# A recurrent layer on one core: the vector engine's mixing-matrix product put ahead of the convolution taps in two steps of every block, and one scan moved from step 123 to step 125

## The chip, the cores and the metric

One core of a Trainium2 chip runs the whole program; the other cores are idle. The metric is the device time in microseconds. The kernel before took 1806.57 us (median of 3 runs, 1805.43 to 1807.76). A difference under 0.2%, 3.6 us, is not told from no change.

## What is computed

Two batches of 1024 tokens with 512 features are normalised, go through a state-space layer (64 heads of 64, state 128, 8 groups) and are gated by a small linear layer. Cut to what matters:

```python
xn = layernorm(x)
gate, hbc, dt = split(xn @ in_proj_w.T)
xBC = silu(conv_bias + sum(pad(hbc)[:, k:k + L] * conv_weight[:, k] for k in range(4)))
x_, B, C = split(xBC)
# step over tokens
state = state * exp(softplus(dt + dt_bias) * A)[..., None, None] + dtx[..., None] * B
y = einsum('bhpn,bhn->bhp', state, C)
# then
yn = rms_norm_per_group(y + x_ * D) * norm_weight * silu(gate)
s = yn @ out_proj_w.T
out = x + s * silu(xn @ W.T + bias + lora(xn))
```

## The kernel before

The recurrence is computed in chunks of 128 tokens: inside a chunk by a mixing matrix, between chunks through the state. A chunk of one group of 8 heads is a **step**; there are N = 128 of them (2 batches x 8 groups x 8 chunks), numbered `i`. Eight steps make one group of heads. Four steps make a **block** of 512 tokens (CPB = 4), the unit of the convolution. TAIL is 124, the first step of the last block.

Every engine's program is one written-out loop over `i`, and each engine works through its own in order, waiting on named semaphores. Nothing reorders them.

What one step holds, by engine (the lines are those of the profile):

- **TensorE (PE)**: the output projection `output` of step i-2 (12 matmuls into `ps_out`), the products L1448 and L1453 that make y of chunk i-1 from its mixing matrix M (`decay`, or `stage` for three of the last chunks) and from the state, the product of B and C into `ps_g` (L1273, L1274), 12 matmuls of a convolution tile, 12 of a gate tile, the state update `ps_s` (L1485), in most steps 12 matmuls of a second convolution tile, and four transposes (L1367).
- **VectorE (DVE)**: `scan` (L990, the running products of the decays, with a small product L997 for the last column), `dtx` and `xw` (L1030, L1038), the sums on y, state and output (L1043, L1049, L1056, L1082), `ynt_lo` (L1086), `taps` (three L875 for one convolution tile) and `mixing_matrix` (L1011: the scanned decays times `ps_g`, which gives M).
- **ScalarE (ACT)**: `conv`, the first tap of a tile and its bias (L643; in the second block of a group of heads with three single columns L642 ahead of it, in the first with a copy of three columns L627), `silu` of the finished tile (L649), the square of y (L793), `ynt_hi` (L809), the gate's silu (L707) and splits of weights. From step 120 on it makes `dtx` and `xw` as well (L770, L799).
- **GpSimd (POOL)**: the products with C (`cpre`, L1203), sums of squares, state decay (L1250), skip (L1258), rest of the weight splits.

The six convolution tiles of the next block are made in the four steps r = i % 4 of the present one. `conv_early(i)` is tile 1, 3, 5 in r = 1, 2, 3, and `conv_late(i)` is tile 0, 2, 4 in r = 0, 1, 2. For each tile PE makes 12 matmuls, ACT the first tap (semaphore `tap0`), DVE three further taps (`taps`), ACT the silu. The early tile's taps stand at the end of DVE's step i, the late tile's at the start of its step i+1. On ACT the silu of the early tile is the last thing in step i, and the first tap of the late tile is the first in step i+1.

In the four steps 0 to 3 of a group of heads the convolution tiles are those of its second block (with the edge columns L642); this text calls them an **edge block**. Steps 4 to 7 make those of the next group's first block (L627): a **plain block**.

In DVE's program M of step i came last, behind the early taps, up to step TAIL. The three last chunks 125, 126, 127 (AHEAD) have their decays in rooms of `stage`, and their scans stand in earlier steps: 127 in step 120, 125 in step 122, 126 in step 123.

Of the kernel before, what the change touches and what calls it, by code (L numbers as in the profile page):

```python
# [22 lines left out]
CPB = BLK // P  # L23
# [8 lines left out]
N = NB * CPB  # L32
# [5 lines left out]
TAIL = N - CPB  # L38
# [25 lines left out]
def inner(i):  # L64

    return (NCH - 1) * (i // NCH) + min(i % NCH, NCH - 2) + 1
# [30 lines left out]
def conv_early(i):  # L97

    nb, r = i // CPB + 1, i % CPB
    return nb * MT + 2 * r - 1 if r and nb < NB else None  # L100
# [49 lines left out]
def by_head(ap):  # L150
    return ap.rearrange("p (h c) -> p h c", h=GH)


def build(nc, hidden, w_in_t, conv_w, conv_b, dt_bias, a_log, d_skip, norm_w, w_out_t,
          lora_a, lora_b_t, w_ffn_t, ffn_bias, lora_w, out):
    ctx = ExitStack()
    with ctx:
# [137 lines left out]
        def decay_room(i):  # L295

            if i in AHEAD:
                at = AHEAD.index(i)
                return stage[1][:, GH * P:] if at == 0 else stage[0][:, (at - 1) * GH * P:at * GH * P]
            return decay[i % 3][:, :]  # L300
# [7 lines left out]
        def lasts(i):  # L308
            return (S["last_ahead"], AHEAD.index(i)) if i in AHEAD else (S["last"], inner(i))

        def scanned(i):
            return (S["scan_ahead"], AHEAD.index(i) + 1) if i in AHEAD else (S["scan"], i + 1)
# [5 lines left out]
        def last_rooms(f):  # L318

            if apart(f):  # L320
                return stage[1][:, 0:DM], stage[1][:, DM:2 * DM], S["landed_io_apart"]
            return io[:, :], x_again[:, :], S["landed_io"]
# [267 lines left out]
        def _(e):  # L590
# [160 lines left out]
            for i in range(N + DRAIN):  # L751
# [79 lines left out]
                if f is not None:  # L831
                    factor, _, landed = last_rooms(f)
                    w.wait_ge(landed, 32 * landings(f))
                    e.activation(factor, factor, ACT.Silu).then_inc(S["ffn_act"], 1)

        @block.vector
        def _(e):
# [30 lines left out]
            def taps(k):  # L868

                nb, m, blk, tile = tile_of(k)  # L870
                ps, acc = ps_conv[k % 2], xc[nb % 2][:, m, :]
                w.wait_ge(S["tap0"], k + 1)
                for d in range(1, TAPS):
                    w.wait_ge(S["taps"], taps_done(k - 1) + d - 1 if d > 1 else 0)
                    e.scalar_tensor_tensor(acc[:, d:], ps[:, 0:BLK - d], convw_sb[:, tile, TAPS - 1 - d:TAPS - d],  # L875
                                           acc[:, d:], ALU.mult, ALU.add).then_inc(S["taps"], 1)
# [76 lines left out]
            def fin(f, sums):  # L953

                acc = out_sum[:, f % NCH, :]
                factor, addend, _ = last_rooms(f)
                w.wait_ge(S["osum"], sums)
                w.wait_ge(S["ffn_act"], f + 1)
                e.tensor_tensor(acc, acc, factor, ALU.mult).then_inc(S["fin1"], 1)
                w.wait_ge(S["fin1"], f + 1)  # L960
                w.wait_ge(S["fin2"], f)
                e.tensor_tensor(acc, acc, addend, ALU.add).then_inc(S["fin2"], 1)
# [22 lines left out]
            def scan(i):  # L985

                d = decay_room(i)
                w.wait_ge(*decays_landed(i))
                w.wait_ge(S["eye"], 2)
                e.tensor_tensor_scan(d, d, eye8[:, :, :].rearrange("p h i -> p (h i)"), 0.0,  # L990
                                     ALU.mult, ALU.add).then_inc(scanned(i)[0], 1)
                if i % NCH < NCH - 1:
                    w.wait_ge(*scanned(i))
                    w.wait_ge(S["xw"], inner(i) - 1 if i <= TAIL else 0)
                    if i in AHEAD:
                        w.wait_ge(landed_prefix[i % NCH], 32)
                    e.tensor_tensor(last_room(i)[:, :, :], by_head(d)[:, :, P - 1:P], step_sizes(i).unsqueeze(2),  # L997
                                    ALU.mult).then_inc(lasts(i)[0], 1)

            def mixing_matrix(i):  # L1000
                u, d = i - DRAIN, decay_room(i)
                w.wait_ge(*scanned(i))
                w.wait_ge(S["mm_g"], i + 1)
                w.wait_ge(S["var2"], u + 1 if u >= 0 else 0)
                if i % NCH < NCH - 1:
                    w.wait_ge(S["b_tok"], inner(i))
                if i < N - 1:
                    w.wait_ge(*lasts(i))
                else:
                    w.wait_ge(S["last"], inner(TAIL))  # L1010
                e.tensor_tensor(by_head(d), by_head(d), ps_g[:, P:2 * P].unsqueeze(1).to_broadcast([P, GH, P]),  # L1011
                                ALU.mult).then_inc(S["M"], 1)

            for i in range(N + DRAIN):
# [75 lines left out]
                    fin_rest(u, f)  # L1090
                if u == N - 2:
                    fin(f, u + 1)
                if i < N and conv_early(i) is not None:
                    taps(conv_early(i))
                if i <= TAIL:
                    mixing_matrix(i)
                for k in {TAIL - 4: (N - 1,), TAIL - 2: (N - 3,), TAIL - 1: (N - 2,)}.get(i, ()):
                    scan(k)

        @block.gpsimd  # L1100
        def _(e):
# [50 lines left out]
            def fin_multiply(f):  # L1152
                b, c = f // NCH, f % NCH
                acc = out_sum[:, c, :]
                factor, _, _ = last_rooms(f)
                w.wait_ge(S["osum"], (b * GROUPS + GROUPS - 1) * NCH + c + 1)
                w.wait_ge(S["ffn_act"], f + 1)
                e.tensor_tensor(acc, acc, factor, ALU.mult).then_inc(S["fin1"], 1)
# [370 lines left out]
```

## Time and profile before

| | us |
|---|---|
| median of 3 runs | 1806.57 (1805.43 to 1807.76) |
| profiled execution, its own time | 1806.44 |
| span of its records | 1804.6 |
| PE busy | 1763.4 (98%) |
| PE weight loads busy | 1421.6 (79%) |
| DVE busy | 1522.1 (84%) |
| POOL busy | 1144.6 (63%) |
| ACT busy | 836.0 (46%) |

The profile is of one execution. Busy time is the time in which an engine has an instruction in work; ends of matmuls are modelled. "Idle before" names what an engine waited for just ahead of an instruction. The time of the profiled execution is its span and 1.8 us around it.

### The profile page before, as it was taken

To read this page: it belongs to the slowest core of one execution; us is meant where nothing else is said; L and a number is where in the kernel's file an instruction comes from. 1 tells how busy PE (TensorE), PEld (TensorE's weight loads), DVE (VectorE), ACT (ScalarE), POOL (GpSimd) and SP (SyncE) were. 2 spreads that over 40 slices of the span, in tenths; PEclk is the share of its full clock that TensorE was granted. 3 is DMA by queue.
4 is the path that set the end of the run, shared out by engine and by line. 5 is a ranking of instruction groups with operands and counts; after the bars stand their busy time and mean duration, and the time that the engine had idled before them with its cause. 6 is when DMAs were issued, how large, how long until landed. Compare 5 with 4: busy or idle time off the path is not lost.

```text
span 1804.6 us, 30682 instructions
## 1 busy us (share of the span) xinstructions
PE 1763.4 (98%) x11416; PEld 1421.6 (79%) x11416; DVE 1522.1 (84%) x1936; ACT 836.0 (46%) x1923; POOL 1144.6 (63%) x1143
## 2 busy tenths in 40 slices
PE   6999999999999999999999999999999999999997
PEld 4777888888888888888877788888888888888875
DVE  6868888888888888888888988889898888989877
ACT  4554354444435344443534444454444435444464
POOL 5428557574755757475697847648574764847466
PEclk9999999999999999999999999999999999999999
DMA  7543333233332423233564333323233332324234
GB/s 253 159 130 110 106 106 140 83 129 106 106 107 105 141 88 123 106 106 110 183 214 155 117 116 122 112 94 123 88 121 113 124 111 95 133 78 139 84 111 146
DMA packets 113508, 220.78 MB, mean 122 GB/s; under 512 B 10448, under 2 KB 46672, under 8 KB 113360
## 3 DMA queue, kind: packets, MB, share of 16 engines
q1 hardware_dynamic: 112320, 218.66, 35.7%
q8 instruction: 91, 1.49, 0.3%
q14 instruction: 57, 0.47, 0.1%
q10 hardware_dynamic: 1040, 0.16, 0.0%
HBM read 204.63 MB, written 14.16 MB: 121 GB/s over the span
## 4 chain that ended last, share of the span: by engine, by line
PE 81%; DVE 7%; ACT 4%; issue 3%; POOL 3%; DMA 1%; SPq 0%; ACTq 0%; DVEq 0%; POOLq 0%
PE ps_conv L1281 9%; PE ps_conv L1284 8%; PE ps_y L1448 6%; PE ps_conv L1287 6%; PE ps_out L1281 6%; PE ps_out L1284 6%; PE ps_gate L1281 6%; PE ps_gate L1284 6%; PE ps_y L1453 5%; PE ps_s L1485 5%; PE ps_out L1287 4%; PE ps_gate L1287 4%; PE turned_x L1367 3%; DVE xc L875 2%; PE ps_conv L1288 2%
## 5 line engine op out<-in xcount | busy, mean ns | idle before, releaser
L875 DVE SCALAR_TENSOR_TENSOR xc<-ps_conv,convw_sb,xc 128x511 f32<-128x511 f32 (+2 forms) x576 | 430.3, 747 | 154.0 <-ACT xc L643 140.5
L1214 POOL TENSOR_TENSOR rstd_col<-mean_square,half 128x1 f32<-128x1 f32 x128 | 90.1, 704 | 535.4 <-ACT mean_square L784 535.4
L990 DVE TENSOR_TENSOR_SCAN decay<-decay,eye 128x1024 f32<-128x1024 f32 x125 | 294.8, 2359 | 1.1 <-DMA decay<-decays_d 1.1
L649 ACT ACTIVATE xc<-xc 128x512 f32<-128x512 f32 x192 | 121.0, 632 | 321.9 <-DVE xc L875 320.5
L1203 POOL TENSOR_TENSOR cpre<-cpre,xc 128x1024 f32<-128x1024 f32 x112 | 268.9, 2401 | 0.0
L1281 PE MATMUL ps_conv<-xn_hi,wconv_hi 128*128 128x512 f32 x768 | 241.9, 437 | 0.0
L1284 PE MATMUL ps_conv<-xn_hi,wconv_lo 128*128 128x512 f32 x768 | 207.4, 392 | 0.0
L1448 PE MATMUL ps_y<-decay,dtx 128*64 128x128 f32 x1984 | 190.9, 279 | 3.3 <-DVE decay L1011 2.5
L1281 PEld LDWEIGHTS ps_conv<-xn_hi,wconv_hi 128*128 128x128 f32 x768 | 141.4, 194 | 49.3 <-issue 27.2
L793 ACT ACTIVATE square<-ps_y 128x512 f32<-128x512 f32 x126 | 75.6, 600 | 224.9 <-DVE ps_y L1043 224.9
L1453 PE MATMUL ps_y<-cpre,state 128*64 128x128 f32 x1760 | 171.1, 273 | 0.0
L1284 PEld LDWEIGHTS ps_conv<-xn_hi,wconv_lo 128*128 128x128 f32 x768 | 144.2, 188 | 33.0
L1287 PE MATMUL ps_conv<-xn_lo,wconv_hi 128*128 128x512 f32 x576 | 162.0, 389 | 0.0
L1448 PEld LDWEIGHTS ps_y<-decay,dtx 128*64 128x64 f32 x1984 | 117.0, 136 | 47.0 <-issue 33.4
L1281 PE MATMUL ps_out<-wout_hi,ynt_hi 128*128 128x512 f32 x512 | 150.4, 415 | 3.3 <-issue 2.1
L1011 DVE TENSOR_TENSOR decay<-decay,ps_g 128x1024 f32<-128x1024 f32 x125 | 151.3, 1210 | 0.7 <-ACT b_tok L777 0.7
L643 ACT ACTIVATE xc<-ps_conv,convb_sb,convw_sb 128x512 f32<-128x512 f32 (+1 forms) x192 | 150.8, 785 | 0.0
L1284 PE MATMUL ps_out<-wout_hi,ynt_lo 128*128 128x512 f32 x512 | 138.4, 392 | 0.0
L1281 PE MATMUL ps_gate<-xn_hi,wgate_hi 128*128 128x512 f32 x504 | 137.9, 395 | 0.0
L1258 POOL TENSOR_TENSOR skip<-xc,dskip_sb 128x512 f32<-128x512 f32 x128 | 133.3, 1042 | 5.8 <-ACT xc L649 5.8
L1284 PE MATMUL ps_gate<-xn_hi,wgate_lo 128*128 128x512 f32 x504 | 135.0, 390 | 0.0
L1086 DVE TENSOR_TENSOR ynt_lo<-ps_y,ynt_hi 128x512 fp32r<-128x512 f32 x126 | 87.1, 691 | 51.8 <-ACT ynt_hi L809 51.0
(235 smaller groups left out, 3909.0 us busy)
## 6 DMA issues: line engine op xcount, KB each, us to landing
decay<-decays_d SPq DMA_DIRECT2D x125, 512.0 KB, 5.2
cpre<-rows_d SPq DMA_DIRECT2D x112, 512.0 KB, 3.9
stage<-w_in_t SPq DMA_DIRECT2D x32, 1024.0 KB, 6.5
stage<-w_out_t SPq DMA_DIRECT2D x16, 1024.0 KB, 5.5
stage<-w_in_t SPq DMA_DIRECT2D x32, 256.0 KB, 3.2
out_sum<-hidden SPq DMA_DIRECT2D x16, 256.0 KB, 5.6
ffn_d<-sgate SPq DMA_DIRECT2D x16, 256.0 KB, 2.3
out<-out_sum SPq DMA_DIRECT2D x16, 256.0 KB, 3.1
```

The costliest lines, as they stand in the source:

```text
L643: e.activation(acc[:, first:], ps[:, first:], ACT.Identity, bias=convb_sb[:, tile, 0:1], scale=tap).then_inc(S["tap0"], 1)
L649: e.activation(xc[nb % 2][:, m, :], xc[nb % 2][:, m, :], ACT.Silu).then_inc(S["silu"], 1)
L875: e.scalar_tensor_tensor(acc[:, d:], ps[:, 0:BLK - d], convw_sb[:, tile, TAPS - 1 - d:TAPS - d], acc[:, d:], ALU.mult, ALU.add).then_inc(S ...
L990: e.tensor_tensor_scan(d, d, eye8[:, :, :].rearrange("p h i -> p (h i)"), 0.0, ALU.mult, ALU.add).then_inc(scanned(i)[0], 1)
L1011: e.tensor_tensor(by_head(d), by_head(d), ps_g[:, P:2 * P].unsqueeze(1).to_broadcast([P, GH, P]), ALU.mult).then_inc(S["M"], 1)
L1203: e.tensor_tensor(cpre[k % 2][:, :, :], cpre[k % 2][:, :, :], xc[i // CPB % 2][:, XT + 1, block_cols(i % NCH)].unsqueeze(1).to_broadcast([ ...
L1258: e.tensor_tensor(turns(skip), xc[nb % 2][:, 0:XT, block_cols(i % NCH)], dskip_sb[:, gi * XT:(gi + 1) * XT].unsqueeze(2).to_broadcast([P, ...
L1281: e.matmul(ps, a_hi(t), b_hi_(t), start=t == 0, stop=False)
L1284: e.matmul(ps, a_lo(t), b_hi_(t), start=False, stop=False)
L1287: e.matmul(ps, a_hi(t), b_lo_(t), start=False, stop=False)
L1448: mixed = e.matmul(y_h, dx[:, h * HD:(h + 1) * HD], mx[:, h * P:(h + 1) * P], start=True, stop=cm == 0, skip_group_check=True)
L1453: mixed = e.matmul(y_h, before[:, h * HD:(h + 1) * HD], c_left[:, h, :], start=False, stop=True, skip_group_check=True)
```

## The change

In steps with r = 1 and r = 2 DVE computes M before the early tile's taps, not after them. In r = 0 (no early tile) and r = 3 the order stays. And the scan of chunk 126 stands at the end of step 125 instead of step 123. No instruction is added or taken away, and the programs of the other engines are as they were.

```diff
@@ -1090,11 +1090,14 @@
                     fin_rest(u, f)
                 if u == N - 2:
                     fin(f, u + 1)
+                matrix_first = i % CPB in (1, 2)
+                if i <= TAIL and matrix_first:
+                    mixing_matrix(i)
                 if i < N and conv_early(i) is not None:
                     taps(conv_early(i))
-                if i <= TAIL:
+                if i <= TAIL and not matrix_first:
                     mixing_matrix(i)
-                for k in {TAIL - 4: (N - 1,), TAIL - 2: (N - 3,), TAIL - 1: (N - 2,)}.get(i, ()):
+                for k in {TAIL - 4: (N - 1,), TAIL - 2: (N - 3,), TAIL + 1: (N - 2,)}.get(i, ()):
                     scan(k)
```

On DVE, from the end of a step with r = 1 or 2 (`ynt_lo`) over the early taps to the late ones; before:

```order
L1086 TENSOR_TENSOR ynt_lo<-ps_y,ynt_hi 128x512
L875 SCALAR_TENSOR_TENSOR xc1<-ps_conv1,convw_sb,xc1 128x511
L875 SCALAR_TENSOR_TENSOR xc1<-ps_conv1,convw_sb,xc1 128x510
L875 SCALAR_TENSOR_TENSOR xc1<-ps_conv1,convw_sb,xc1 128x509
L1011 TENSOR_TENSOR decay1<-decay1,ps_g 128x1024
L875 SCALAR_TENSOR_TENSOR xc1<-ps_conv0,convw_sb,xc1 128x511
L875 SCALAR_TENSOR_TENSOR xc1<-ps_conv0,convw_sb,xc1 128x510
L875 SCALAR_TENSOR_TENSOR xc1<-ps_conv0,convw_sb,xc1 128x509
```

and now:

```order
L1086 TENSOR_TENSOR ynt_lo<-ps_y,ynt_hi 128x512
L1011 TENSOR_TENSOR decay1<-decay1,ps_g 128x1024
L875 SCALAR_TENSOR_TENSOR xc1<-ps_conv1,convw_sb,xc1 128x511
L875 SCALAR_TENSOR_TENSOR xc1<-ps_conv1,convw_sb,xc1 128x510
L875 SCALAR_TENSOR_TENSOR xc1<-ps_conv1,convw_sb,xc1 128x509
L875 SCALAR_TENSOR_TENSOR xc1<-ps_conv0,convw_sb,xc1 128x511
L875 SCALAR_TENSOR_TENSOR xc1<-ps_conv0,convw_sb,xc1 128x510
L875 SCALAR_TENSOR_TENSOR xc1<-ps_conv0,convw_sb,xc1 128x509
```

M (L1011) stood between the early tile's taps (`ps_conv1`) and the late tile's (`ps_conv0`); now these six stand side by side, with M ahead.

On DVE at the end of step 123 and the start of step 124; before:

```order
L1011 TENSOR_TENSOR decay0<-decay0,ps_g 128x1024
L990 SCALAR_TENSOR_TENSOR stage0<-stage0,eye8 128x1024
L997 TENSOR_TENSOR last2<-stage0,prefix_dt 128x8
L990 SCALAR_TENSOR_TENSOR decay1<-decay1,eye8 128x1024
L997 TENSOR_TENSOR last0<-decay1,prefix_dt 128x8
```

and at the end of step 125 and the start of step 126, now:

```order
L976 TENSOR_TENSOR ps_out<-ps_out,stage1 128x512
L979 TENSOR_TENSOR out_sum<-ps_out,stage1 128x512
L990 SCALAR_TENSOR_TENSOR stage0<-stage0,eye8 128x1024
L997 TENSOR_TENSOR last2<-stage0,prefix_dt 128x8
L1043 TENSOR_TENSOR ps_y<-ps_y,skip 128x512
```

L990 is the scan (the trace calls it TENSOR_TENSOR_SCAN). The scan of chunk 126 and its L997 have left the place ahead of the scan of chunk 124 (`decay1`), and stand ahead of step 126's first sum on y.

## Rows read from the trace of the kernel before

**Rows 1.** The page, part 1: busy time, share of the span, instructions

```profile
PE 1763.4 (98%) x11416; PEld 1421.6 (79%) x11416; DVE 1522.1 (84%) x1936; ACT 836.0 (46%) x1923; POOL 1144.6 (63%) x1143
```

**Rows 2.** Windows, one group: us, busy by engine, granted clock, DMA

```profile
1175.04:1280.08 105.04, 105.04 (x694) 85.09 (x693) 90.38 (x114) 47.47 (x107) 66.26 (x67) 1.00 0.33 111
```

**Rows 3.** Who waited for L1011 (M); waits of PE's weight loads: us, times, longest

```profile
  PEld ps_y L1448: 14.3, 32
...
PEld ps_y L1448 <- issue: 33.6, 94, 1.2
```

**Rows 4.** Timeline of DVE, edge block, steps 81 to 83: start, us, what

```profile
1195.14 2.31 DVE L875 SCALAR_TENSOR_TENSOR xc<-ps_conv,convw_sb,xc 128x511 f32<-128x511 f32 x3
1197.37 1.21 DVE L1011 TENSOR_TENSOR decay<-decay,ps_g 128x1024 f32<-128x1024 f32 x1
1199.55 2.32 DVE L875 SCALAR_TENSOR_TENSOR xc<-ps_conv,convw_sb,xc 128x511 f32<-128x511 f32 x3 [0.97 <-ACT xc L643]
...
1214.07 2.32 DVE L875 SCALAR_TENSOR_TENSOR xc<-ps_conv,convw_sb,xc 128x511 f32<-128x511 f32 x3 [1.29 <-ACT xc L643]
...
1226.10 1.21 DVE L1011 TENSOR_TENSOR decay<-decay,ps_g 128x1024 f32<-128x1024 f32 x1
1227.22 0.68 DVE L1030 TENSOR_TENSOR dtx<-turned_x,prefix_dt 128x512 f32<-128x512 f32 x1
```

**Rows 5.** Timeline of ACT beside it, step 81 to 82

```profile
1197.48 0.63 ACT L649 ACTIVATE xc<-xc 128x512 f32<-128x512 f32 x1 [2.49 <-DVE xc L875]
1198.02 0.82 ACT L642 ACTIVATE xc<-ps_conv,edge,convw_sb 128x1 f32<-128x1 f32 x3
1198.73 0.78 ACT L643 ACTIVATE xc<-ps_conv,convb_sb,convw_sb 128x509 f32<-128x509 f32 x1
```

**Rows 6.** Timeline of PE's weight loads: y of chunks 3, 67 and 83

```profile
170.78 0.20 PEld L1448 LDWEIGHTS ps_y<-decay,dtx 128*64 128x64 f32 x4 [0.94 <-DVE decay L1011]
...
1017.51 0.20 PEld L1448 LDWEIGHTS ps_y<-decay,dtx 128*64 128x64 f32 x4 [1.41 <-DVE decay L1011]
...
1227.59 0.20 PEld L1448 LDWEIGHTS ps_y<-decay,dtx 128*64 128x64 f32 x4 [0.35 <-DVE decay L1011]
```

**Rows 7.** Timeline of ACT, plain block: the late tiles of steps 85, 86

```profile
1251.21 0.18 ACT L627 ACTIVATE tails<-ps_conv 128x3 f32<-128x3 f32 x1 [1.17 <-PE ps_conv L1288]
...
1265.95 0.17 ACT L627 ACTIVATE tails<-ps_conv 128x3 f32<-128x3 f32 x1 [1.40 <-PE ps_conv L1288]
```

**Rows 8.** Timeline of DVE, late taps after M of steps 2, 62, 65

```profile
157.49 2.32 DVE L875 SCALAR_TENSOR_TENSOR xc<-ps_conv,convw_sb,xc 128x511 f32<-128x511 f32 x3 [0.97 <-ACT xc L643]
...
949.54 2.31 DVE L875 SCALAR_TENSOR_TENSOR xc<-ps_conv,convw_sb,xc 128x511 f32<-128x511 f32 x3 [0.83 <-ACT xc L643]
...
988.97 2.32 DVE L875 SCALAR_TENSOR_TENSOR xc<-ps_conv,convw_sb,xc 128x511 f32<-128x511 f32 x3 [1.49 <-ACT xc L643]
```

**Rows 9.** Timeline of DVE, the tail: steps 123, 124 and 126

```profile
1755.39 1.21 DVE L1011 TENSOR_TENSOR decay<-decay,ps_g 128x1024 f32<-128x1024 f32 x1
1756.52 2.28 DVE L990 TENSOR_TENSOR_SCAN stage<-stage,eye 128x1024 f32<-128x1024 f32 x1
...
1759.83 2.28 DVE L990 TENSOR_TENSOR_SCAN decay<-decay,eye 128x1024 f32<-128x1024 f32 x1
...
1785.85 0.70 DVE L976 TENSOR_TENSOR ps_out<-ps_out,io 128x512 f32<-128x512 f32 x1 [1.38 <-ACT io L834]
```

**Rows 10.** Timeline of PE, the tail: y of chunk 123, state updates 124, 125

```profile
1756.65 0.44 PE L1448 MATMUL ps_y<-decay,dtx 128*64 128x128 f32 x4 [1.00 <-DVE decay L1011]
...
1766.16 2.04 PE L1485 MATMUL ps_s<-xw,b_tok 128*128 128x512 f32 x2 [4.25 <-ACT xw L801]
...
1775.27 1.10 PE L1485 MATMUL ps_s<-xw,b_tok 128*128 128x512 f32 x2
```

**Rows 11.** Windows in the tail (columns as in rows 2)

```profile
1766.00:1768.00 2.00, 1.84 (x2) 0.73 (x3) 1.42 (x2) 1.56 (x4) 1.92 (x3) 0.50 0.00 0
```

**Rows 12.** Line L990 (the scans): shortest, median and longest, ns

```profile
L990 DVE TENSOR_TENSOR_SCAN decay<-decay,eye x125: 2277/2281/3199, 120.3 to 1759.8; 128x1024 f32<-128x1024 f32 x125
```

## The prediction

> **What bounds the kernel now.** I read the page's busy times first, then windows, then who waits for M, then the timelines of DVE, ACT and PE beside each other.
>
> PE is busy 98% of the span and DVE 84% [rows 1]. One group of heads, eight steps, takes 105.04 us, and PE is busy for all 105.04 of them [rows 2]; the group before it takes the same time. So in the middle of the program PE sets the pace.
>
> The question is how far DVE is behind it. Over the whole run PE's weight loads waited for M 14.3 us in 32 places [rows 3]. But for one, these are y of a block's fourth step (r = 3), three of which are shown [rows 6]. There PE has the least work between the step's start and its need of M, since r = 3 has no late tile. M of chunk 83 ends at 1226.10 + 1.21 = 1227.31 and the weight load for its y starts at 1227.59 [rows 4, 6]. Where PE really waits, the load starts 0.05 us after M's end: M of chunk 123 ends at 1756.60, y starts at 1756.65 [rows 9, 10]. So in an edge block DVE has 0.28 - 0.05 = 0.23 us to spare at r = 3, and no more. The reader is to see this: DVE looks idle for 16% of the time, but its chain through steps 1 to 3 of a block is as long as PE's.
>
> What does this chain consist of? In r = 1 the early taps start at 1195.14 and M at 1197.37. Then the late taps start at 1199.55, after 0.97 us of idle time that ends with ACT's first tap [rows 4]. ACT could not be sooner: the silu of the early tile starts at 1197.48, just behind the early taps, then the edge columns at 1198.02, the first tap at 1198.73, and DVE's late taps at 1199.55 [rows 5]. From the end of the early taps to the start of the late ones is 2.18 us of ACT's work, whatever DVE does meanwhile. In the kernel before, M fills 1.21 of it.
>
> **The change, part by part.**
>
> *M ahead of the early taps, edge block, r = 1.* M takes 1.12 us of DVE's queue (1226.10 to 1227.22 [rows 4]). The early taps start with no idle time before them, so they slide by 1.12. Behind them ACT's silu slides, and its first tap of the late tile is queued behind that silu. The 2.18 us are now bare idle time on DVE. The late taps start 1.12 us later.
>
> *The same, r = 2.* Before, M of chunk 82 ends at 1214.07 - 1.29 = 1212.78 and began 1.21 before, at 1211.57, the end of the early taps [rows 4]. From there to the late taps are 2.50 us, 0.32 more than 2.18: here PE's late tile came last. Now it is 1.12 + 2.18 = 3.30 instead of 2.50: 0.80 later.
>
> All that DVE does in the next step hangs on the late taps' end, without a gap that could absorb it; its one idle time there, for `ynt_hi`, follows DVE's own y. So M at r = 3 comes 1.12 + 0.80 = 1.92 us later, and y on PE by 1.92 - 0.23 = 1.7 us. Behind this y stands all of PE's queue. M at r = 1 and r = 2 comes earlier, which nobody waits for.
>
> *Plain block.* There ACT stood idle for 1.17 and 1.40 us before the late tile, until PE had finished it [rows 7]. The silu may slide by 1.12 within both. Cost nothing; if PE were faster there, 1.12 would show.
>
> *How many.* Groups 1 to 7 and 9 to 14 are alike, 13 x 1.7 = 22.1. Group 0: both idle times are 0.97 (one shown [rows 8]), so both steps cost 1.12, and y of chunk 3 waited 0.94 already [rows 6], so nothing is to spare: 2.2. Group 8: y of chunk 67 waited 1.41 [rows 6]; one of its two steps has 1.49 idle [rows 8], so costs 0.6, the other 1.12: 1.7. Group 7 has a plain block whose second late tile waited only 0.83 [rows 8], less than M itself: ACT was last, not PE, and the step costs 1.1. Sum 22.1 + 2.2 + 1.7 + 1.1 = 27.1 us.
>
> *The tail.* In group 15 the step r = 1 costs 1.12 again; in r = 2 the scan of chunk 125 covers ACT's work. So M of chunk 123 is 1.1 late, and y with it, since it waited already [rows 10]. Then the scan of 126 is gone: the scan of 124 followed it after 1759.83 - 1756.52 = 3.31 us [rows 9]. It now comes 3.31 - 1.12 = 2.2 us sooner. PE waited 4.25 us for `xw` behind that scan [rows 10], so it gains the 2.2. In step 125 the scan comes back, 2.4 to 3.3 us ahead of step 126. It is paid from two places: DVE's wait of 1.38 for a transfer at 1785.85 [rows 9], and its wait for the transfer of step 125, both of which are issued sooner by what PE gained. The clock speaks for more: after the 4.25 us without matmuls the state update took 2.04 us against 1.10 a step later [rows 10], at a granted clock of 0.50, the 1.2 GHz level [rows 11]. With a wait near 1 us this may not occur. Bounds: +1.1 (the scan lies wholly on the path twice over) and -4.6 (2.2, and some 2.4 from the clock). I take -2.2, since the transfers' waits are there to be filled.
>
> The trace has scans of up to 3.20 us against a median of 2.28 [rows 12], so a scan can be held up by at most 0.9 us here. The Trainium skill (SBUF — State Buffer, "Who interferes with whom") says that a DVE instruction with two SBUF inputs and a GpSimd one that reads SBUF lock each other out for a whole instruction. By it the scan in step 125 could wait for the whole of a GpSimd product, and the tail's gain would be gone; that agrees in kind with the 3.20, and lies within my bounds.
>
> Sum: 27.1 - 2.2 = +24.9 us. The profiled execution took 1806.4, so 1831.3. It stands 0.1 us from the median of the runs, which I leave out.
>
> **The rivals.**
>
> 1. *Only half shows.* One of the two slides is absorbed, for instance since PE's late tile is last in r = 2 anyhow. Then an edge block costs 1.12 - 0.23 = 0.9: some 14 us over 15 groups, less 2, gives 1818. Against it: 0.32 of PE's share there is already taken off.
>
> 2. *It feeds on itself.* DVE stays late relative to PE in the plain block, and its cover of 1.17 is used up. Then the plain block costs up to 0.8 + 1.1 as well: 3.6 a group, 15 groups, about 1858. Against it: PE is late by 1.7 too, DVE by 1.92, and the plain block starts with r = 0, where DVE has idle time.
>
> 3. *Nothing shows.* The ends of matmuls are modelled, and the true slack at r = 3 may be above 1.9. Then 1804 to 1808. Against it: M's end and y's start are 0.28 apart in the edge blocks, and y of 67 and 3 did wait.
>
> 4. *Faster: M is the wall.* The weight loads' 14.3 us of waits for M [rows 3] vanish as M comes sooner: 1792.1. It decides if y at r = 1 and 2 starts with M's end rather than with PE's own row. For it speaks that DVE's M is the only thing named before y. Against it: the waits are at r = 3, where M is not moved, and most of them last 0.35 us [rows 6], which is also the mean gap before y where nothing was waited for, 33.6 us over 94 places [rows 3]. The Trainium skill (Trainium Kernel Development and Optimization, "Performance Expectations") calls matmul busy time a bad measure and weight-load busy time a good one. By it PE, with weight loads busy at 79%, would have room, and this rival would be the likeliest; the row of a group with PE busy all 105.04 us can't refute this alone, but groups of equal length can be had only from an engine that never waits for something that varies.
>
> **How the numbers follow.** The forecast has 0.77, rival 1 has 0.08, rival 2 has 0.04, rival 3 has 0.07, rival 4 has 0.04. A measurement of this kernel tells 0.2%, 3.6 us, from no change. Faster is rival 4: 0.04. Same is rival 3: 0.07. Slower is the rest: 0.89. The low end of the range is rival 1's, 1818. The high end is no slack anywhere, 15 x 1.92 + 2.2 us, and the tail at +1.1: some 1839, and a little for y's dependence on `cpre`, which comes on POOL just before: 1840.
>
> **What would show it.** Right: DVE's idle time before the late taps is near 2.1 us after steps 1 and 2 of edge blocks, against 0.97 and 1.29; the weight load before y of an r = 3 chunk in an edge block waits some 1.7 us more for M (L1011); plain blocks keep their 52.5 us (half a group [rows 2]); edge blocks take 54.2; the scan of 124 starts 2.2 us sooner after M of 123 than before, counted with the delay; the state update of step 124 waits for 1 to 2 us. Wrong: edge blocks of unchanged length (rival 3), plain blocks longer (rival 2), or M's waits gone altogether (rival 4).

## The result, and the profile after

| | before | after |
|---|---|---|
| device time, median | 1806.0 us (1805.28 to 1807.76, 4 runs) | 1833.44 us (1831.46 to 1834.84, 4 runs) |
| profiled execution, its span | 1806.4 us, 1804.6 us | 1834.75 us, 1832.9 us |
| one group of heads | 105.04 us [rows 2] | 106.73 us |

The ratio is 1.0152, 95% interval 1.0140 to 1.0164: slower by 27.4 us. 1831.3 had been forecast, in a range of 1818 to 1840. In the changed kernel all helper lines stand three lines lower (L1448 is L1451, L1281 is L1284, L1485 is L1488); M is L1011 and the taps are L875, as before.

The page of the changed kernel, parts 1 and 4 (busy times; the chain that ended last, shares by engine), to be held against [rows 1]:

```profile
PE 1769.0 (97%) x11416; PEld 1420.8 (78%) x11416; DVE 1520.9 (83%) x1936; ACT 827.0 (45%) x1923; POOL 1175.2 (64%) x1143
...
PE 39%; DVE 32%; ACT 16%; issue 9%; POOL 2%; DMA 1%; SPq 0%; DVEq 0%; ACTq 0%; POOLq 0%
```

The counts of instructions are those of before. POOL is busy for 30.6 us longer and PE for 5.6; the instructions are the same, some of them took longer. What changed is the chain: DVE and ACT now hold 48% of it, against 11% in the page of the kernel before, since PE waits in each edge block for what they make.

Windows of the changed kernel: the edge block of a steady group, its plain block, and both (columns as in rows 2).

```profile
1193.41:1247.65 54.24, 52.87 (x341) 42.28 (x340) 44.33 (x58) 27.59 (x64) 32.61 (x33) 1.00 0.28 96
1247.65:1300.14 52.49, 52.49 (x353) 42.76 (x354) 46.02 (x57) 19.19 (x43) 36.08 (x35) 1.00 0.36 123
1193.41:1300.14 106.73, 105.36 (x694) 85.04 (x694) 90.35 (x114) 46.78 (x107) 68.69 (x67) 1.00 0.32 109
```

The same two blocks in the kernel before:

```profile
1175.04:1227.59 52.55, 52.55 (x341) 42.33 (x340) 44.57 (x58) 28.17 (x64) 30.61 (x33) 1.00 0.30 101
1227.59:1280.08 52.49, 52.49 (x354) 42.76 (x353) 45.81 (x57) 19.31 (x43) 35.65 (x35) 1.00 0.36 121
```

The edge block takes 54.24 us, and PE is idle in it for 1.37; the plain block takes its 52.49 and PE is busy throughout. So the loss lies in the edge block alone, 106.73 - 105.04 = 1.69 us a group.

DVE in that edge block, steps 81 to 83, beside [rows 4]:

```profile
1213.50 1.21 DVE L1011 TENSOR_TENSOR decay<-decay,ps_g 128x1024 f32<-128x1024 f32 x1
1214.63 2.31 DVE L875 SCALAR_TENSOR_TENSOR xc<-ps_conv,convw_sb,xc 128x511 f32<-128x511 f32 x3
1219.03 2.32 DVE L875 SCALAR_TENSOR_TENSOR xc<-ps_conv,convw_sb,xc 128x511 f32<-128x511 f32 x3 [2.09 <-ACT xc L643]
...
1234.37 2.32 DVE L875 SCALAR_TENSOR_TENSOR xc<-ps_conv,convw_sb,xc 128x511 f32<-128x511 f32 x3 [2.09 <-ACT xc L643]
...
1244.16 2.31 DVE L875 SCALAR_TENSOR_TENSOR xc<-ps_conv,convw_sb,xc 128x511 f32<-128x511 f32 x3
1246.39 1.21 DVE L1011 TENSOR_TENSOR decay<-decay,ps_g 128x1024 f32<-128x1024 f32 x1
```

ACT beside it, first step, and PE's weight load for the y of chunk 83:

```profile
1216.97 0.63 ACT L649 ACTIVATE xc<-xc 128x512 f32<-128x512 f32 x1 [3.63 <-DVE xc L875]
1217.51 0.82 ACT L642 ACTIVATE xc<-ps_conv,edge,convw_sb 128x1 f32<-128x1 f32 x3
1218.22 0.78 ACT L643 ACTIVATE xc<-ps_conv,convb_sb,convw_sb 128x509 f32<-128x509 f32 x1
```

```profile
1247.65 0.20 PEld L1451 LDWEIGHTS ps_y<-decay,dtx 128*64 128x64 f32 x4 [1.41 <-DVE decay L1011]
```

And the one other stop of PE in this edge block, at the output projection just ahead of that y:

```profile
1243.67 1.17 PE L1284 MATMUL ps_out<-wout_hi,ynt_hi 128*128 128x512 f32 x4 [0.39 <-ACT ynt_hi L809]
```

M now stands first, the early taps end 1.12 us later, ACT's silu starts right behind them at 1216.97, and the late taps' first tap comes third in ACT's queue. DVE is idle for 2.09 us in both steps, where it had been idle for 0.97 and 1.29 [rows 4]. M of chunk 83 ends at 1246.39 + 1.21 = 1247.60, and the weight load starts 0.05 later, where it had started 0.28 after M [rows 4, 6].

PE loses the 1.69 us at two places. Counted from the start of the edge block, the output projection starts 50.26 us in, against 49.62 before (its first matmul was at 1224.66 there): 0.64 us late, for `ynt_hi`, which hangs on DVE's sums on y. The other 1.05 are the wait for M.

Who waited for M in the changed kernel, and what ACT's silu waited for (us, times, longest). In the kernel before, this view gives 13.6 us in 31 places for M; the 14.3 in 32 of [rows 3] hold one more, for a chunk in `stage`.

```profile
PEld ps_y L1451 <- DVE decay L1011: 28.9, 31, 1.4
ACT xc L649 <- DVE xc L875: 404.8, 186, 3.6
```

The end of the changed kernel: PE's state updates and y, then DVE's two last scans, then POOL.

```profile
1784.60 0.44 PE L1451 MATMUL ps_y<-decay,dtx 128*64 128x128 f32 x4 [1.00 <-DVE decay L1011]
1790.83 1.10 PE L1488 MATMUL ps_s<-xw,b_tok 128*128 128x512 f32 x2 [0.97 <-issue]
...
1798.43 1.10 PE L1488 MATMUL ps_s<-xw,b_tok 128*128 128x512 f32 x2
...
1809.09 2.05 PE L1488 MATMUL ps_s<-xw,b_tok 128*128 128x512 f32 x2 [2.98 <-ACT xw L801]
```

```profile
1784.46 2.28 DVE L990 TENSOR_TENSOR_SCAN decay<-decay,eye 128x1024 f32<-128x1024 f32 x1
...
1802.49 2.59 DVE L990 TENSOR_TENSOR_SCAN stage<-stage,eye 128x1024 f32<-128x1024 f32 x1
1805.11 0.82 DVE L997 TENSOR_TENSOR last<-stage,prefix_dt 128x8 f32<-128x8 f32 x1
```

```profile
1802.88 3.03 POOL L1261 TENSOR_TENSOR skip<-xc,dskip_sb 128x512 f32<-128x512 f32 x1
```

Behind that scan, DVE's sum on y of chunk 125, and what ACT did when it was there:

```profile
1806.02 0.70 DVE L1043 TENSOR_TENSOR ps_y<-ps_y,skip 128x512 f32<-128x512 f32 x1
```

```profile
1806.75 0.60 ACT L793 ACTIVATE square<-ps_y 128x512 f32<-128x512 f32 x1 [2.92 <-DVE ps_y L1043]
1807.24 1.54 ACT L799 ACTIVATE xw<-turned_x,last 128x64 f32<-128x64 f32 x7
```

Windows there, just before the last of these state updates and from it on:

```profile
1807.00:1809.00 2.00, 0.00 (x0) 0.00 (x0) 1.92 (x3) 2.00 (x10) 2.00 (x2) 0.83 1.00 382
1809.00:1811.00 2.00, 1.91 (x3) 0.80 (x4) 2.00 (x4) 0.99 (x2) 1.92 (x4) 0.50 0.53 203
```

The wait of 4.25 us and the long state update of [rows 10] are gone from step 124, as forecast (0.97 us are left of the wait, 1 to 2 were forecast); but a wait of 2.98 and a state update of 2.05 us now stand in step 126, behind the scan that was put back. And this scan overlaps a product on POOL that took 3.03 us, against 1.04 for the same product elsewhere.

### The profile page after: what moved, and what is told of

The parts are those of the page before. It is cut to its first block, busy times and chain, and to the rows that moved or that the text cites. A ratio compares the mean times of both kernels' runs of the same rounds, so it can differ in the third digit from the quotient of the medians.

```text
span 1832.9 us, 30682 instructions
## 1 busy us (share of the span) xinstructions
PE 1769.0 (97%) x11416; PEld 1420.8 (78%) x11416; DVE 1520.9 (83%) x1936; ACT 827.0 (45%) x1923; POOL 1175.2 (64%) x1143
## 3 DMA queue, kind: packets, MB, share of 16 engines
q8 instruction: 91, 1.49, 0.3%
## 4 chain that ended last, share of the span: by engine, by line
PE 39%; DVE 32%; ACT 16%; issue 9%; POOL 2%; DMA 1%; SPq 0%; DVEq 0%; ACTq 0%; POOLq 0%
DVE xc L875 11%; DVE decay L990 8%; PE ps_conv L1284 4%; PE ps_conv L1287 4%; DVE decay L1011 4%; ACT xc L643 4%; ACT xc L642 4%; PE ps_y L1451 3%; PE ps_conv L1290 3%; PE ps_y L1456 3%; DVE ps_y L1043 2%; PE ps_out L1284 2%; PE ps_gate L1284 2%; PE ps_gate L1287 2%; PE ps_out L1287 2%
## 5 line engine op out<-in xcount | busy, mean ns | idle before, releaser
L875 DVE SCALAR_TENSOR_TENSOR xc<-ps_conv,convw_sb,xc 128x511 f32<-128x511 f32 (+2 forms) x576 | 430.5, 747 | 184.4 <-ACT xc L643 170.8
L1217 POOL TENSOR_TENSOR rstd_col<-mean_square,half 128x1 f32<-128x1 f32 x128 | 124.0, 969 | 531.3 <-ACT mean_square L784 531.3
L990 DVE TENSOR_TENSOR_SCAN decay<-decay,eye 128x1024 f32<-128x1024 f32 x125 | 294.3, 2354 | 0.9 <-DMA decay<-decays_d 0.9
L1206 POOL TENSOR_TENSOR cpre<-cpre,xc 128x1024 f32<-128x1024 f32 x112 | 268.4, 2396 | 0.0
L1284 PE MATMUL ps_conv<-xn_hi,wconv_hi 128*128 128x512 f32 x768 | 241.9, 437 | 0.0
L1451 PE MATMUL ps_y<-decay,dtx 128*64 128x128 f32 x1984 | 190.9, 279 | 17.6 <-DVE decay L1011 16.8
L1284 PEld LDWEIGHTS ps_conv<-xn_hi,wconv_hi 128*128 128x128 f32 x768 | 141.4, 194 | 49.3 <-issue 29.8
L1451 PEld LDWEIGHTS ps_y<-decay,dtx 128*64 128x64 f32 x1984 | 117.0, 136 | 62.4 <-issue 33.4
L1284 PE MATMUL ps_out<-wout_hi,ynt_hi 128*128 128x512 f32 x512 | 150.3, 415 | 7.4 <-ACT ynt_hi L809 6.2
L1011 DVE TENSOR_TENSOR decay<-decay,ps_g 128x1024 f32<-128x1024 f32 x125 | 151.3, 1210 | 0.6 <-ACT b_tok L777 0.6
L1284 PE MATMUL ps_gate<-xn_hi,wgate_hi 128*128 128x512 f32 x504 | 138.0, 395 | 0.0
L1253 POOL TENSOR_TENSOR state<-state,total_bc 128x512 f32<-128x512 f32 x96 | 130.1, 1355 | 0.0
```

Source lines behind the costliest of these rows:

```text
L1206: e.tensor_tensor(cpre[k % 2][:, :, :], cpre[k % 2][:, :, :], xc[i // CPB % 2][:, XT + 1, block_cols(i % NCH)].unsqueeze(1).to_broadcast([ ...
L1253: e.tensor_tensor(by_head(dec[:, :]), by_head(new[:, :]), heads_bc(total_bc[:, first:first + GH]), ALU.mult).then_inc(S["sdec"], 1)
L1284: e.matmul(ps, a_hi(t), b_hi_(t), start=t == 0, stop=False)
L1451: mixed = e.matmul(y_h, dx[:, h * HD:(h + 1) * HD], mx[:, h * P:(h + 1) * P], start=True, stop=cm == 0, skip_group_check=True)
```

## The experiments

The theory on record: what costs is the order of ACT's queue. The late tile's first tap stands behind the early tile's silu, and the silu behind the early taps; whatever is put ahead of the early taps slides the late ones, once the 2.18 us of ACT's chain are bare. The rivals: the scan's place carries the loss; M's place does, by PE waiting for M itself; DVE is simply too full.

Each edit is told against the changed kernel or against the kernel before; `matrix_first` is the changed kernel's condition. In the runs that edit this condition the scan of 126 stands in step 123, as in the kernel before, unless the edit shows another step. "Before" is each time the kernel before on the same chip.

**The two parts apart.** First M's order alone, with the scan of 126 back in step 123:

```diff
-for k in {..., TAIL + 1: (N - 2,)}.get(i, ()):
+for k in {..., TAIL - 1: (N - 2,)}.get(i, ()):
```

> M ahead of the early taps in r = 1 and 2, the scan of chunk 126 left in step 123. Queue theory (the silu of the early tile and the first tap of the late one hang behind the early taps): y of chunk 119 is 26.8 us later than in the kernel before, as in the changed kernel, and the tail adds 1.1 us, so 1806.0 + 28 = 1834, ratio 1.0155. Rival (the moved scan makes up a good part of the loss): under 1825. The idle time before the late taps in edge blocks is 2.1 us after both steps.

Measured 1834.0 us (1833.6 to 1834.51), ratio 1.0158 [1.0144, 1.0172], as the queue theory had it. All of the loss is here.

Then the scan alone, with M behind the taps in every step:

```diff
-for k in {..., TAIL - 1: (N - 2,)}.get(i, ()):
+for k in {..., TAIL + 1: (N - 2,)}.get(i, ()):
```

> The scan of chunk 126 alone moved to the end of step 125, M after the taps everywhere. From the changed kernel's tail, where step 124 gained 3.8 us and steps 126 and 127 gave back 4.4: between 1804 and 1807, no change to be told, y of chunk 119 as in the kernel before (1700.2). The lower end if PE's wait for the state update of step 126 stays short enough that the granted clock does not fall, the upper if it falls. Rival (the scan's return is wholly hidden, as predicted blind): 1802.7, since step 124 starts without the 1.1 us of delay.

Measured 1805.27 us against 1805.91, ratio 0.9995 [0.9987, 1.0004]: nothing that can be told. The state updates of PE in its profile:

```profile
1762.88 1.10 PE L1485 MATMUL ps_s<-xw,b_tok 128*128 128x512 f32 x2 [0.95 <-issue]
...
1781.13 1.41 PE L1485 MATMUL ps_s<-xw,b_tok 128*128 128x512 f32 x2 [2.96 <-ACT xw L801]
```

The first, of step 124, starts 3.28 us sooner than the one of 1766.16 in [rows 10]. The one of step 126 waits 2.96 us, where no wait had been. The scan's move takes back what it gives, with or without M first.

**One of the two steps alone.** M first at r = 1 only, the scan as before:

```diff
-matrix_first = i % CPB in (1, 2)
+matrix_first = i % CPB in (1,)
```

> M first in r = 1 only, scan of 126 in step 123. Queue theory: an edge block costs 1.12 - 0.23 = 0.9 us, 13 of them 11.6, group 0 1.1, group 8 0.6, the tail 1.1: 1806.0 + 14.4 = 1820.4. Plain blocks keep 52.49 us. Rival (every M moved costs its own 1.2 us of DVE time, wherever it stands): 32 steps, 38 us, 1844. Rival (the loss comes only if both steps are moved): 1806.

Measured 1815.65 us (1815.25 to 1816.99), ratio 1.0057 [1.0042, 1.0073]. That is below what was expected. A group of it, and the two late taps of its edge block:

```profile
1075.73:1181.35 105.62, 105.14 (x694) 85.14 (x694) 90.41 (x114) 46.84 (x107) 68.17 (x67) 1.00 0.32 110
```

```profile
1206.97 2.32 DVE L875 SCALAR_TENSOR_TENSOR xc<-ps_conv,convw_sb,xc 128x511 f32<-128x511 f32 x3 [2.09 <-ACT xc L643]
...
1221.17 2.32 DVE L875 SCALAR_TENSOR_TENSOR xc<-ps_conv,convw_sb,xc 128x511 f32<-128x511 f32 x3 [0.96 <-ACT xc L643]
```

The group loses 0.58 us. The idle time of r = 2 shrank from 1.29 to 0.96: the 0.32 us by which PE was last there are DVE's own slack too, and they absorb part of a slide that comes from r = 1. 1.12 - 0.32 - 0.23 = 0.57. The expectation had forgotten this, while the prediction of the whole change had the 0.32 in its step for r = 2.

M first at r = 2 only:

```diff
-matrix_first = i % CPB in (1, 2)
+matrix_first = i % CPB in (2,)
```

> M first in r = 2 only, scan of 126 in step 123. Queue theory: PE's late tile came 0.3 us after ACT was free there, so an edge block costs 0.80 - 0.23 = 0.57 us, 12 of them 6.8, group 7 0.6 and 1.1 for its plain block, group 0 and 8 1.1 each, the tail nothing since the scan of chunk 125 covers it: 1806.0 + 10.7 = 1816.7. Rival (the same price as for r = 1): 1820. Rival (each M moved costs 1.2 us): 1844.

Measured 1816.3 us (1815.5 to 1818.49), ratio 1.0061 [1.0048, 1.0075], as expected; its group takes 105.62 as well, 0.80 - 0.23 = 0.57. The halves sum to 1.16 a group and the whole is 1.69: slack is spent once, so 0.23 + 0.32 = 0.55 us are saved twice when the halves are measured apart.

**Where ACT has room.** M first only in steps 5 and 6 of a group, the plain block:

```diff
-matrix_first = i % CPB in (1, 2)
+matrix_first = i % NCH in (5, 6)
```

> M first only in steps 5 and 6 of a group of heads (plain blocks), scan of 126 in step 123. Queue theory: ACT's waits of 1.17 and 1.40 us for PE cover the 1.12; only the plain block of group 7 pays 1.0. 1807, no change to be told; idle time before the late taps falls from 1.59 and 1.82 to 1.43 and 1.8 counted behind the taps. Rival (all of the loss is not special to the edge blocks): 1820.

Measured 1806.51 us against 1805.12, ratio 1.0006 [0.9996, 1.0015], no change, as expected; one group, from the y of chunk 71 to that of 79, took 105.04. Only the plain block of group 7 paid, 0.95 us from the y of chunk 59 to that of 63. The same reordering on the same engine costs nothing where the late tile comes from PE later than ACT's chain ends.

**ACT's order turned round.** The changed kernel, and on ACT the late tile's first tap ahead of the early tile's silu:

```diff
+if conv_early(m) is not None:
+    silu(conv_early(m))
 silu(conv_late(m))
...
-if conv_early(i) is not None:
+if conv_early(i) is not None and conv_late(i) is None:
     silu(conv_early(i))
```

> The changed kernel, and on ACT the first tap of the late tile ahead of the silu of the early tile, in r = 1 and 2. Queue theory: the late taps no longer hang behind the early taps, they come with PE's late tile as before (idle time before them about 1.0 us in edge blocks), the edge block is back at 52.55 us and y of chunk 119 near 1700.2. With the tail of the changed kernel (+0.4 or -2): 1804 to 1807. Rival (the early taps' later end holds the bank of ps_conv or DVE's queue itself, not ACT's order): 1833 as the changed kernel.

Measured 1800.67 us (1799.27 to 1801.19) against 1805.12, ratio 0.9969 [0.9958, 0.9980]: 4.5 us below the kernel before, and so some 32 below the changed one. The return to the old time was expected; that it would go below it was not, and the next run tells why. ACT in its step 81, a group of it, and DVE's late taps there:

```profile
1194.63 0.84 ACT L642 ACTIVATE xc<-ps_conv,edge,convw_sb 128x1 f32<-128x1 f32 x3 [2.81 <-PE ps_conv L1293]
1195.36 0.78 ACT L643 ACTIVATE xc<-ps_conv,convb_sb,convw_sb 128x509 f32<-128x509 f32 x1
1196.02 0.64 ACT L649 ACTIVATE xc<-xc 128x512 f32<-128x512 f32 x1
```

```profile
1066.85:1171.89 105.04, 105.04 (x694) 85.09 (x693) 90.40 (x114) 47.07 (x107) 65.93 (x67) 1.00 0.34 111
```

```profile
1196.17 2.32 DVE L877 SCALAR_TENSOR_TENSOR xc<-ps_conv,convw_sb,xc 128x511 f32<-128x511 f32 x3 [0.75 <-ACT xc L643]
```

ACT's first tap now waits for PE's last convolution matmul and for nothing of DVE's. M stands first, and the group is PE's 105.04 again. DVE is as full as in the changed kernel (90.40 against 90.35 us in a group), so "DVE is too full" falls, and the order of ACT's queue is shown as the cause of the group's loss.

ACT's order alone: the edit above, with M behind the taps and the scan in step 123 as in the kernel before.

```diff
-if i <= TAIL and matrix_first:
-    mixing_matrix(i)
...
-if i <= TAIL and not matrix_first:
+if i <= TAIL:
```

> The order of the kernel before on DVE (M behind the taps in every step, the scan of 126 in step 123), and on ACT the first input step of the next late tile ahead of the early tile's activation. Theory: the steady group is PE's own 105.04 us already, so nothing is won there; late taps come up to 1 us sooner, and with them M in the stretches where PE waits for it (chunks 3, 67, 123: 0.94, 1.41, 1.00 us): 1802.5 to 1804.5. Rival (the change of ACT's order gives nothing by itself, and the 1800.7 of the run with both comes from M being early): 1804.5 to 1806.

Measured 1801.77 us (1800.42 to 1803.67) against 1806.16, ratio 0.9978 [0.9969, 0.9987], a little below the 1802.5 to 1804.5 of the theory. PE's weight load for the y of chunk 67, which waited 1.41 us before [rows 6]:

```profile
1013.97 0.20 PEld L1450 LDWEIGHTS ps_y<-decay,dtx 128*64 128x64 f32 x4 [0.35 <-DVE decay L1013]
```

Against [rows 6, 10], y of chunk 3 starts 0.76 us sooner in this profile, of chunk 67 3.54, of chunk 123 4.68. So nearly all of the gain is ACT's order by itself, in the stretches where a group isn't regular. With M first (1800.67) it may be a microsecond better, which isn't told apart.

**M first where PE does wait for it.** All of r = 1, 2 and 3:

```diff
-matrix_first = i % CPB in (1, 2)
+matrix_first = i % CPB in (1, 2, 3)
```

> M first in r = 1, 2 and 3, scan of 126 in step 123. M of r = 3 then stands 2.2 us sooner in DVE's queue, more than the 1.7 it was late. Queue theory: the wait for M vanishes, but DVE stays 1.9 us behind, and ynt_hi (0.6 us late in the changed kernel) becomes what PE waits for in an edge block, and DVE's delay runs on into the plain block: a loss of 0.6 to 1.2 us a group, 1815 to 1824. Rival (y's wait for M is the whole matter): 1806.

Measured 1830.49 us (1828.06 to 1832.43), ratio 1.0137 [1.0123, 1.0151]; a group is 106.39. A miss: I had expected 1815 to 1824, most of the loss gone with M off the path. DVE's M of step 83, then PE, and the wait that took over:

```profile
1239.76 1.21 DVE L1011 TENSOR_TENSOR decay<-decay,ps_g 128x1024 f32<-128x1024 f32 x1
```

```profile
1239.26 1.17 PE L1284 MATMUL ps_out<-wout_hi,ynt_hi 128*128 128x512 f32 x4 [0.39 <-ACT ynt_hi L809]
...
1242.90 0.44 PE L1451 MATMUL ps_y<-decay,dtx 128*64 128x128 f32 x4 [0.66 <-POOL cpre L1206]
```

```profile
PE ps_y L1451 <- POOL cpre L1206: 11.2, 17, 1.1
```

M ends at 1240.97, 1.9 us before y, and y is late all the same: PE waits for `ynt_hi` of ACT and for `cpre` of POOL, which come late too. What POOL did before `cpre`, and DVE beside it:

```profile
1233.33 2.08 POOL L1217 TENSOR_TENSOR rstd_col<-mean_square,half 128x1 f32<-128x1 f32 x1 [7.66 <-ACT mean_square L784]
```

```profile
1232.79 2.28 DVE L990 TENSOR_TENSOR_SCAN decay<-decay,eye 128x1024 f32<-128x1024 f32 x1
```

POOL had stood 7.66 us for ACT's `mean_square`, which is queued on ACT behind the late tile's silu. Then its product on one column, which takes 0.55 us where no scan runs, took 2.08 and ended 0.34 us after DVE's scan. So `cpre` follows DVE's scan, and this scan is as late as the late taps ahead of it.

M was the operand that came last in the changed kernel, and not the only one that was late. `cpre` of the same chunk ended there at 1247.18 (L1206 at 1244.78, for 2.40), 0.42 before M; y starts 0.15 after `cpre` here, so an estimate of what M's absence can give is 1247.65 - 1247.33 = 0.32 us. Taking M away gave back 1.69 - 1.35 = 0.34 us a group.

r = 3 alone, the one place where the kernel before waits for M:

```diff
-matrix_first = i % CPB in (1, 2)
+matrix_first = i % CPB in (3,)
```

> M ahead of the early taps in the fourth step of a block only (r=3), the scan of 126 back in step 123. The only waits of PE for M that the kernel before has are at chunks whose M is made in such a step (0.94, 1.41 and 1.00 us at chunks 3, 67 and 123), and M now ends about 2.2 us sooner there. Theory (the wait for M is what PE has left to lose, and the 1.12 us that the early taps' input step takes longer falls where no late tile follows): these three waits go, minus 2 to 3 us, 1802 to 1803.5. Rival (M is no wall even there, another operand is late by nearly as much): 1804.5 to 1806. Rival (the early tile's activation on ACT, 1.12 us later, holds the gate work behind it): slower, 1807 or more.

Measured 1803.67 us (1802.84 to 1804.89) against 1806.16, ratio 0.9988 [0.9979, 0.9997]: 2.5 us less, as the theory had it. That is less than the 3.6 that this measurement was said to tell, though the interval leaves out 1.

**The scan one step sooner.** The kernel before, with the scan of 126 in step 124:

```diff
-TAIL - 1: (N - 2,)
+TAIL: (N - 2,)
```

> The kernel before with the scan of chunk 126 at the end of step 124, where DVE stood idle for 3.69 us until y of chunk 124 was there. The scan and L997 (2.4 to 3.3 us) fit into that gap as it moves. Step 124 gains 3.3 to 3.8 us and nothing is given back: 1802.5, 0.2% faster, and no clock drop behind step 124. Rival (the gap closes as step 124 moves up, and the scan delays y of chunk 124 on DVE by 1 to 2 us): 1804 to 1805.

Measured 1803.3 us (1802.63 to 1804.53) against 1805.12, ratio 0.9989 [0.9980, 0.9998]: 1.8 us less, between the theory (1802.5) and its rival (1804 to 1805). Its state updates of steps 124, 125 and 126:

```profile
1761.24 1.10 PE L1485 MATMUL ps_s<-xw,b_tok 128*128 128x512 f32 x2 [0.97 <-issue]
...
1770.82 1.10 PE L1485 MATMUL ps_s<-xw,b_tok 128*128 128x512 f32 x2 [2.03 <-ACT xw L801]
...
1779.49 1.10 PE L1485 MATMUL ps_s<-xw,b_tok 128*128 128x512 f32 x2 [1.00 <-issue]
```

The longest wait for `xw` is 2.03 here, in step 125, against 4.25 in step 123's version [rows 10] and 2.96 in step 125's, and no state update is a long one.

With M first at r = 3 as well:

```diff
-matrix_first = i % CPB in (1, 2)
+matrix_first = i % CPB in (3,)
...
-TAIL + 1: (N - 2,)
+TAIL: (N - 2,)
```

> The same, with the scan of chunk 126 at the end of step 124. The run with that scan alone in step 124 measured 1803.3 against 1805.1. If the two gains lie in different stretches they add up: 1800.3 to 1801.7. If both only take the one wait at the step of chunk 123, whichever comes first takes it: 1802 to 1803.5.

Measured 1802.61 us (1801.84 to 1805.35) against 1806.16, ratio 0.9983 [0.9974, 0.9992]: 3.6 us less, where the two gains sum to 4.3. The interval holds both, so the times don't tell whether the gains add up; in absolute time the result lies in the rival's range, but the kernel before took 1806.16 beside it and not the 1805.1 that the expectation started from. Nor do the profiles bear out the rival's reason. In that of r = 3 alone the wait for `xw` in step 124 grew from 4.25 to 5.33 us: what M gave at chunk 123 was waited off a step later, with the scan still in its old place. With both changes this wait is 2.05 us, 3.28 less, just what the scan's move takes off without M first (4.25 to 0.97); but the state update behind it took 2.04 us and not 1.10. Whether that is more than the chance of one profile isn't shown.

With ACT's order turned round and M first at r = 1 and 2:

```diff
 matrix_first = i % CPB in (1, 2)
...
-TAIL + 1: (N - 2,)
+TAIL: (N - 2,)
```

> The changed kernel with ACT's order turned round (measured 1800.67), and the scan of chunk 126 at the end of step 124 instead of 125. From the y of chunk 123 to that of 127 the run with the scan in 125 took 33.2 us, the run with it in 124 took 31.9 us. Theory (in 125 the scan holds the y of chunk 125 on DVE and so PE's state update): 1.0 to 1.6 us less, 1799.1 to 1799.7. Rival (with M early the end is bound elsewhere): 1800.2 to 1801.2.

Measured 1799.94 us (1799.28 to 1800.14) against 1806.16, ratio 0.9967 [0.9955, 0.9980]. It lies between the two expectations, and is the fastest of all, by 0.7 us against the one with the scan in 125 (they were measured beside different runs of before, whose ratios are 0.9967 and 0.9969, so that the two aren't told apart).

## Why the prediction was right, and where it was not

*PE sets the pace, with 0.23 us to spare for DVE at r = 3.* Right. The weight load starts 0.05 us after M in the changed kernel, and 1.69 us a group is 1.92 - 0.23. The halves (0.58 each) and the turned order (back to 105.04) fit the same slack. One sign named for it failed: the weight load was to wait 1.7 us more for M, and it waits 1.41 - 0.35 = 1.06 more. PE had lost the other 0.64 us already, at the output projection, for `ynt_hi`. The prediction named `ynt_hi` as a wait of DVE and left out that PE reads it too. The sum isn't touched, since both hang on the same slide.

*ACT's chain of 2.18 us is bare; 1.12 at r = 1 and 0.80 at r = 2.* Right: both late taps follow an idle time of 2.09 us, and ACT's silu, edge columns and first tap stand as forecast.

*The plain block is free.* Right: 52.49 us, and no change with M first in plain blocks alone.

*The count.* The y of chunk 119 was to come 27.1 us later. It comes at 1727.08 instead of 1700.24, 26.8 later; that profile was 0.60 us ahead of the one before by step 1 already (M of chunk 1 starts at 138.29, where the early taps had started at 138.89), so the change cost 27.4. The terms: group 0, 2.2 forecast, 1.66 + 0.60 = 2.3 found; groups 1 to 6, 1.70; group 7, 2.2 instead of 1.7 in its edge block, since there the second step slid by its full 1.12 (idle 1.49 before, 2.61 after) and not by 0.80; its plain block 1.0 against 1.1; group 8, 1.6 against 1.7. In group 8 the sum came out by luck: the step with an idle time of 1.49, priced at 0.6, slid by the full 1.12 there too (its late taps start 4.92 us after the early ones in both profiles), and the other, priced at 1.12, by 0.5.

*The tail.* Here a term failed: -2.2 was forecast, and from the y of chunk 119 to the end of the span the profile shows 28.3 - 26.8 = +1.5, above even the bound of +1.1. The first part held: y of chunk 123 lost its 1.1, and the scan of 124 started right behind M, so that it was 24.6 us late (1784.46 against 1759.83 [rows 9]), 2.2 less than the 26.8 of chunk 119, as forecast; the y of chunk 124 was 24.1 late. The step that failed is "since the transfers' waits are there to be filled". The scan in step 125 did not only fill a wait of DVE's: DVE's sum on y of chunk 125 is queued behind it and started at 1806.02, ACT's square and `xw` behind that (1806.75, 1807.24), and PE's state update behind `xw`. This `xw` also reads what the moved scan makes, the `last2` of L997, ready at 1805.93, so that another order on ACT could have saved no more than 1.3 us. PE waited 2.98 us for `xw`, and the long state update came back with this wait. I had looked at what DVE waited for, and not at who waited for DVE, although the very same chain was the reason for the gain one step earlier. From y of chunk 125 to y of 126 the changed kernel fell back from 24.1 to 27.5 us late. The run with the scan alone shows the same pair, a wait gone and a wait new, and no change of time. In the medians the tail's miss is smaller than in the profile: 27.4 us were lost, with 24.9 forecast. Of the four runs two took 1831.46 and 1832.13 us at a mean granted clock of 0.998, two 1834.75 and 1834.84 at 0.995 and 0.997; the profile is of one of the latter. That the clock's fall at the end makes this difference is argued from these numbers, and no run settles it.

On the scan of step 125 the prediction weighed a rule of the Trainium skill (SBUF — State Buffer, "Who interferes with whom"), by which such a scan and a GpSimd product lock each other out. The trace agrees in kind, but the product had to wait, not the scan: the scan started first and took 2.59 us against a median of 2.28, the product beside it 3.03 against 1.04, and L997 behind the scan 0.82 against a median of 0.17. Scan and L997 held DVE for 3.53 us (1802.49 to 1806.02), where an undisturbed pair takes 2.51 (1237.20 to 1239.71). The `skip` of chunk 125, which DVE's sum on y reads, ended at 1805.91, as late as L997. So 3.53 - 2.51, some 1.0 us of PE's wait of 2.98, is an estimate of the lock's share. In its old place the pair had cost 3.31 us [rows 9], so the pair costs 0.2 us more than in the kernel before; no run separates it from the scan's place.

*The rivals.* Half shows (1818): it didn't. Each half of the change alone is near 1816, the two together are not. Feeds on itself (1858), nothing shows (1804 to 1808): excluded by the windows. M is the wall (1792.1): there is a kernel in it, but a small one. M first at r = 3 alone gives 2.5 us, not 14.3; 0.35 us of each wait was PE's normal gap, as the prediction argued. Had the range for that rival been worked from the three long waits, 3.35 - 3 x 0.35 = 2.3 us, it would have been right. The Trainium skill (Trainium Kernel Development and Optimization, "Performance Expectations") was cited for this rival: it calls matmul busy time a bad measure, and weight-load busy time a good one, of how close a kernel is to roofline. How close PE is to that, no run here shows. As a sign of which engine sets the pace, the weight loads' 79% would have misled beside DVE's 84%, and the matmuls' 98% did not: with DVE's waits added or taken away, the steady group of eight of the twelve kernels of the experiments is 105.03 to 105.05 us, whatever the order on DVE and ACT, and that of none is shorter.

## What to carry to other kernels

Before an instruction is moved ahead in one engine's queue, follow what is pushed back to the engine that consumes it, and look what stands behind the consumer in *its* queue: the cost here was a first tap on an idle ACT (45% busy) that waited behind a silu for data it did not need, and a change in ACT's order gave back 32 us where DVE's order had lost 28. A slack between two engines is spent once for a whole chain, so halves of a change measured alone don't sum. Where an instruction is put back in a place at which its engine waits, ask who is queued behind it there.

## What the runs showed of the hardware

A small product of GpSimd that starts while a scan of DVE runs ends with the scan. In all fourteen profiles, each of the products `rstd_col` (128 x 1, 128 in a profile) that starts during a scan ends 0.33 to 0.36 us after the scan's end, and takes up to 2.48 us by it (changed kernel); each of the others takes 0.54 to 0.56 us. So a part of POOL's busy time is waiting, and a later scan makes POOL later.

After a wait without matmuls PE's next work ran at full speed in some cases and at half in others, and the length of the wait didn't decide it. The state update took 1.10 us after 2.03 us of waiting (scan in step 124, M behind the taps), and 2.05 us after 2.98 (the changed kernel, granted clock 0.50, the 1.2 GHz level). These two would suggest a limit between them, but the same instruction took 1.41 us after 2.96 (scan alone), and in the profiles of the turned order it took 2.03 us after 2.01, and 1.10 after 2.95:

```profile
1767.39 2.03 PE L1490 MATMUL ps_s<-xw,b_tok 128*128 128x512 f32 x2 [2.01 <-ACT xw L803]
```

```profile
1776.84 1.10 PE L1490 MATMUL ps_s<-xw,b_tok 128*128 128x512 f32 x2 [2.95 <-ACT xw L803]
```

The first is of the kernel with the scan in step 124 (granted clock 0.50 over it), the second of that with the scan in step 125 (1.00 over it). The longer waits differ likewise: 2.04 us after 4.25 in the kernel before [rows 10], 1.10 after 4.23 with M first in plain blocks only. A short state update does not mean that the clock stayed up: in the second profile above the granted clock was 0.54 from 1778 to 1780 us, just behind it. Only with the scan in step 124 and M behind the taps was it still 1.00 from 1772 to 1776, behind the update of 1770.82. So removing one such wait can't be priced with the clock's part included as if it were certain; the gain of 2.4 us in the prediction's lower bound is of this kind.
